# Three attention stages: projections into other PSUM banks, a minimum in place of score masks in level 0, and an order of its own for each level

## The reference

```python
# level 0: causal softmax attention        (level 2: the same without the mask, with its own layer norm)
q, k, v = (einsum('bsd,hdk->bhsk', x, W) + b for each of q, k, v)
scores = q @ k.T / sqrt(8)
scores = where(triu(ones, k=1), -1e9, scores)
out = (softmax(scores) @ v) @ Wo + bo
# level 3: rotated numerator, unrotated denominator, mask after the division
num = exp(rotate(q) @ rotate(k).T * scale)
den = sum(exp(q @ k.T * scale), axis=-1)        # over all keys
out = (where(tril, num / den, 0) @ v) @ Wout + bout
# around each:  x = x + attention(layernorm(x))
```

## Time and profile before

| | us |
|---|---|
| median of three runs | 5368.52 |
| the profiled execution | 5368.35 |
| its span | 5366.6 |
| level 0 attention, from first load to last addition | 274.2 to 502.9 |
| level 2 attention | 2768.7 to 3004.4 |
| level 3 attention | 4953.3 to 5176.4 |

### The profile page before, as it was taken

The page is one execution under the profiler, slowest core; times in us unless marked ns, Lnnn a source line. Parts: engine busy times, 40 slices in busy tenths (PEclk is TensorE's granted clock), DMA queues, the critical chain, the costliest instruction groups (busy, mean ns, idle before and its releaser), DMA issues. The chain is left out here.

```text
span 5366.6 us, 141783 instructions
## 1 busy us (share of the span) xinstructions
PE 4978.9 (93%) x49044; PEld 3454.0 (64%) x49044; DVE 3814.0 (71%) x7030; ACT 3438.1 (64%) x5879; POOL 2867.6 (53%) x3451
## 2 busy tenths in 40 slices
PE   8988977499999999999969699999999999989889
PEld 5655655267777777777745367777777777756556
DVE  2243236488888888888856488888888888845545
ACT  3333323278888888888845378888888888832642
POOL 0010005378788778778720288777787787700200
PEclk9989988599999999999979799999999999989899
DMA  1000000011111111112100111111111111110000
GB/s 44 1 5 34 1 1 9 29 45 55 51 50 51 55 51 49 51 51 55 43 15 1 40 39 55 51 51 49 55 51 55 46 55 51 39 34 7 1 25 9
DMA packets 110454, 195.51 MB, mean 36 GB/s; under 512 B 21409, under 2 KB 28849, under 8 KB 110257
## 3 DMA queue, kind: packets, MB, share of 16 engines
q1 hardware_dynamic: 110256, 192.82, 12.8%
HBM read 53.29 MB, written 1.05 MB: 10 GB/s over the span
## 5 line engine op out<-in xcount | busy, mean ns | idle before, releaser
L2674 POOL TENSOR_TENSOR stage_qk<-stage_halves 128x1024 f32<-128x1024 f32 x384 | 906.0, 2359 | 53.3 <-DVE stage_halves L2790 45.8
L2710 POOL TENSOR_TENSOR stage_qk<-stage_qk,stage_rnorm 128x1024 f32<-128x1024 f32 x384 | 730.9, 1903 | 30.5 <-issue 0.3
L2703 POOL TENSOR_TENSOR stage_probs<-stage_probs,stage_rsum 128x768 f32<-128x768 f32 x384 | 565.3, 1472 | 222.1 <-DVE stage_rsum L2819 209.6
L2787 DVE TENSOR_TENSOR stage_halves<-stage_wide,stage_tables 128x1024 f32<-128x1024 f32 x384 | 468.2, 1219 | 227.6 <-ACT stage_square L2493 187.4
L2493 ACT ACTIVATE stage_square<-stage_wide 128x1024 f32<-128x1024 f32 x384 | 394.0, 1026 | 191.9 <-PE stage_wide L2259 191.5
L2325 PE MATMUL stage_pv<-stage_probsT,stage_v_win 96*64 96x64 f32 x12288 | 488.1, 227 | 2.7 <-ACT stage_ctxT L2546 1.6
L2790 DVE TENSOR_TENSOR stage_halves<-stage_wide,stage_tables 128x512 f32<-128x512 f32 x768 | 490.5, 680 | 0.0
L2325 PEld LDWEIGHTS stage_pv<-stage_probsT,stage_v_win 96*64 96x64 f32 x12288 | 408.4, 137 | 122.7 <-issue 98.5
L2799 DVE TENSOR_REDUCE stage_norm<-stage_square 128x16 f32<-128x1024 f32 x384 | 464.7, 1210 | 30.8 <-issue 30.7
L2276 PE MATMUL stage_turn<-ident,stage_qk 128*128 128x128 f32 x3072 | 478.9, 279 | 4.9 <-ACT stage_qkT L2513 4.7
L2311 PEld LDWEIGHTS stage_flip<-ident,stage_probs 128*96 128x96 f32 x3072 | 355.6, 126 | 194.3 <-issue 130.0
(11 more groups left out here) (299 smaller groups left out, 9877.6 us busy)
## 6 DMA issues: line engine op xcount, KB each, us to landing
stage_v_win<-stage_v SPq DMA_DIRECT2D x384, 192.0 KB, 2.5
stage_v_win<-stage_v SPq DMA_DIRECT2D x384, 128.0 KB, 2.4
stage_v_win<-stage_v SPq DMA_DIRECT2D x192, 64.0 KB, 2.2
stage_wq<-in_T_wq SPq DMA_DIRECT2D x12, 512.0 KB, 4.1
stage_wk<-in_T_wk SPq DMA_DIRECT2D x12, 512.0 KB, 4.7
stage_wv<-in_T_wv SPq DMA_DIRECT2D x12, 512.0 KB, 3.5
stage_wo<-in_T_wo SPq DMA_DIRECT2D x12, 512.0 KB, 3.5
stage_w_up<-in_L_w_up SPq DMA_DIRECT2D x8, 512.0 KB, 6.6
```

The lines of the kernel that those rows point to most:

```text
L2674: nc.gpsimd.tensor_tensor(qk[:, n, :], halves[:, n % 2, 0, :], halves[:, n % 2, 1, :], ALU.add)\
L2703: nc.gpsimd.tensor_tensor(probs[:, m % 2], probs[:, m % 2], rsum[:, m % 2].to_broadcast([P, 2, 2 * HALVES, REACH]), ALU.mult)\
L2710: nc.gpsimd.tensor_tensor(heads, heads, rnorm[:, n, :].rearrange("p (h o) -> p h o", o=1).to_broadcast([P, LH, LD]), ALU.mult).then_inc(at ...
L2787: nc.vector.tensor_tensor(out[:, 0], heads, cos.to_broadcast([P, LH, LD]), ALU.mult)
```

## The change

1. **Banks.** `project` writes q and k to `pvT`. In level 3 the two swapped projections become a piece of their own, `project_swapped`, that writes to `turn`. `duo` then holds scores only. Waits follow: `weigh(…, 0)` waits for the projection to be read, `project` for `copy_weighed(…, 1)`, and the users of `turn` for `rotate` in level 3.
2. **Level 0.** `score` has no mask matmuls. The exponential is taken of all scores, and a new DVE piece, `keep_past`, takes the minimum of the two diagonal 128x128 blocks of each head with a constant (0 above the diagonal, the largest float on it and below). `weigh` waits for that (`kept`) and not for `probs`. `first_score` in level 0 and `score` in level 3 still write their masks by matmul.
3. **Orders.** Each level has its own `body` on each engine.
4. In level 3 `divide` waits for the sums of its own half only, and `read_projection` no longer waits for the scores three steps back (`rotate` does).

```diff
+    if level == 0:
+        per.update(kept=PAIRS)
...
+    usable = "kept" if cut else "probs"
...
+        diagonals = probs[:, :, :].rearrange("p h (b s) -> p h b s", s=P)[:, :, 0:3:2, :]
...
-                for n, w in enumerate([wq, wk] if softmax else [wq, wk, tiles["wq_swap"], tiles["wk_swap"]]):
-                    ins = nc.tensor.matmul(duo[:, n // 2, (n % 2) * SEQ:(n % 2 + 1) * SEQ], w[:, :], xT[:, :], start=True, stop=True)
+                for n, w in enumerate((wq, wk)):
+                    ins = nc.tensor.matmul(pvT[:, n, :], w[:, :], xT[:, :], start=True, stop=True)
                 ins.then_inc(sig["proj"], 1)
+
+            def project_swapped(step):
+                pe.wait_ge(*sig("xT", step, 1))
+                for n, w in enumerate((tiles["wq_swap"], tiles["wk_swap"])):
+                    ins = nc.tensor.matmul(turn[:, n * SEQ:(n + 1) * SEQ], w[:, :], xT[:, :], start=True, stop=True)
+                ins.then_inc(sig["swapped"], 1)
...
-                if causal:
+                if causal and not cut:
                     for side in range(2):
                         nc.tensor.matmul(kinds2(duo[:, side, :])[:, :, 0:P], ident_bf[:, :],
...
-                pe.wait_ge(*sig("probs", step, 2 * g + 2))
+                pe.wait_ge(*sig(usable, step, 2 * g + 2))
...
+            def keep_past(step, n):
+
+                dve.wait_ge(*sig("probs", step, n + 1))
+                own = diagonals[:, 2 * n:2 * n + 2]
+                limits = tiles["limits"].rearrange("p (h t s) -> p h t s", h=1, t=1).to_broadcast([P, 2, T, P])
+                nc.vector.tensor_tensor(own, own, limits, ALU.min).then_inc(sig["kept"], 1)
...
-                    dve.wait_ge(*sig("den", step, GROUPS))
+                    dve.wait_ge(*sig("den", step, 2 * half + 2))
...
+    a["A0_limits"] = np.where(above.T < 0, 0.0, np.finfo(np.float32).max).astype(np.float32)
```

More of the change, by code:

```diff
@@ L791 @@
 _last = [("bo", D), ("wo", D)]
[L792 removed]
+ATTN_PARTS = {0: _every + _softmax + [("limits", P)] + _last, 2: [("gamma", 1), ("beta", 1)] + _every + _softmax + _last,
               3: _every + [("wq_swap", D), ("wk_swap", D), ("rope", 2 * SEQ)] + _last}
@@ L866, in _, with bank_free @@
         def _(pe):
[L867 to L874, removed]
+            def bank_free(*before):
                 for name, step, count in before:
@@ L958, in score @@
                         ins = nc.tensor.matmul(duo[:, side, t * SEQ:(t + 1) * SEQ - first], key[:, t * P:(t + 1) * P],
-                                               query[:, first:SEQ], start=not causal, stop=True, skip_group_check=True)
+                                               query[:, first:SEQ], start=not causal or cut, stop=True, skip_group_check=True)
                 ins.then_inc(sig["scores"], 1)
@@ L1069, in _ @@
+            for s in range(-3, B + 3):
                 body(s)
@@ L1078, in copy_xT @@
                 act.wait_ge(*sig("v_psum", step))
+                if not softmax:
+                    act.wait_ge(*sig("swapped", step))
                 if level == 2:
@@ L1089, in read_projection @@
                     act.wait_ge(*sig("first_scores", step - ROOM + 1))
-                    act.wait_ge(*sig("scores", step - ROOM + 1))
+                    if softmax:
+                        act.wait_ge(*sig("scores", step - ROOM + 1))
                 if softmax:
@@ L1093, in read_projection @@
                         for n, (to, bias) in enumerate(((q_heads, tiles["bq"]), (k_heads, tiles["bk"]))):
-                            ins = nc.scalar.activation(to[:, step % ROOM, g, :], duo[:, 0, n * SEQ:(n + 1) * SEQ], ACT.Identity,
+                            ins = nc.scalar.activation(to[:, step % ROOM, g, :], pvT[:, n, :], ACT.Identity,
                                                        bias=bias[:, g:g + 1], scale=heads_of[:, g:g + 1])
@@ L1097, in read_projection @@
                 else:
-                    nc.scalar.activation(flat[:, step % ROOM, 0:2, :], kinds2(duo[:, 0, :]), ACT.Copy).then_inc(sig["flat"], 1)
+                    nc.scalar.activation(flat[:, step % ROOM, 0:2, :], pvT[:, :, :], ACT.Copy).then_inc(sig["flat"], 1)
             def denominators(step, g):
@@ L1205, in _, with body @@
                 nc.gpsimd.memset(v[:, :, :, :, DK:DK + 1], 1.0).then_inc(once["set"], 1)
-            def body(s):
-                if not softmax and runs(s):
-                    only_heads(s, 0)
-                if runs(s + 3):
-                    deviation(s + 3)
-                if not softmax and runs(s):
-                    only_heads(s, 1)
-                if runs(s + 2):
-                    add_bias(s + 2)
-                if level == 2 and runs(s + 3):
-                    second_deviation(s + 3)
-            for s in range(-3, B):
+            if level == 0:
+                def body(s):
+                    if runs(s + 2):
+                        add_bias(s + 2)
+                    if runs(s + 3):
+                        deviation(s + 3)
+            elif level == 2:
+                def body(s):
+                    if runs(s - 2):
+                        add_bias(s - 2)
+                    if runs(s):
+                        deviation(s)
+                    if runs(s - 1):
+                        second_deviation(s - 1)
+            else:
+                def body(s):
+                    if runs(s - 3):
+                        add_bias(s - 3)
+                    if runs(s + 1):
+                        only_heads(s + 1, 0)
+                    if runs(s + 1):
+                        only_heads(s + 1, 1)
+                    if runs(s + 3):
+                        deviation(s + 3)
+            for s in range(-3, B + 3):
                 body(s)
```

535 lines of the change are left out of this document (396 added, 139 removed).

## The result

The kernel after takes 5289.57 us (median of four runs, 5286.48 to 5293.0), the kernel before 5371.74 in the same comparison: a ratio of 0.9855, 95% interval 0.9839 to 0.9871. The forecast was 5294 us. The profiled execution took 5288.43 us, 79.9 less than that of before.

The account below looks back on a forecast made before the run. PE led, with waits from an equally long chain through `duo`. Savings of 16 us in fills, 42.4 in even steps and 15.9 in drains, 74.3 in all, took 5368.35 to 5294 us, range 5280 to 5306.

Parts of the forecast that it names:

- Banks, with the order: Projection leaves `duo`, so PE's work bounds even steps: 19.5, 21.6, 21.7 us in levels 0, 2, 3, masks' removal included.
- tight fit at `weigh(., 0)`: Level 0: last head copy ends about 5.6 us after the projection, and PE reaches the weighing 5.6 us after it.
- Masks to minima: Level 0's even steps: 2.6 us of masks leave PE per step; DVE gets eight minima, 5.5 us.
- DVE's slack: Level 0's even steps: DVE comes to 17.0 us of work (16.3 to 19.0) in a step of 19.5 us.
- Fills, level 0: Start of level 0, until step 3's projection: masks go, one piece comes, 3 us saved (bounds -4 and 12).
- the rival that I gave 0.17: Full clock comes sooner in fills or level 2's drain, each saving 7.5 us: 5272 us; chance 0.17.
- Fill, level 3: Five of ten first scores move behind step 3's projection, about 1.1 us each at half clock: 11 us saved (0 to 18).
- Drains: From step 7's projection on: 12.5 us saved in level 0, 6 in level 2, 2.6 lost in level 3.
- the projection's hold goes as well: Drains: the projection no longer occupies `duo`, saving 5.0 us in level 0, 5.5 in level 2, 5.2 in level 3.
- DVE did not lead: First rival: DVE leads in level 0, a step takes about 21.5 us, half a us more elsewhere: 5316 us; chance 0.15.
- `pvT` was no chain: Rival: PE stands at `weigh(., 0)` for head copies each step, so only masks' 21 us are saved: 5350 us; chance 0.08.
- the clock rose to 1.00 instead of falling: Rival: level 0's clock falls once full mask matmuls leave, a step costing 18.9 us more: 5389 us; chance 0.05.

Follow-up runs that it names:

- banks_only: Kernel before with q and k projections of levels 0 and 2 sent to `pvT`, every engine's old order kept: 5403.9 us, 1.006 of before.
- duo_again: Kernel after with the projections of levels 0 and 2 back in `duo` under the new order: 5414.16 us, 1.0083 of before.
- masks_back: Kernel after with level 0's score masks written by matmul again and no minima: 5316.85 us, 0.9894 of before.
- min_twice: Kernel after with every minimum of level 0 done twice, first into a spare tile: 5307.23 us, 0.9905 of before.
- min_only: Kernel before with level 0's score masks replaced by minima on DVE, old banks and PE order: 5356.35 us, 0.9971 of before.
- ahead3: Kernel after with level 3's first scores, their exponentials and sums one step earlier: 5310.12 us, 0.9898 of before.
- warm_first: Kernel after without level 0's first-score masks, with unread matmuls in level 0's fill and drain and level 2's fill: 5268.5 us, 0.9816 of before.
- warm: Kernel after with unread matmuls where PE would stand in fills and drains of levels 0 and 2: 5295.79 us, 0.988 of before.

## Why the prediction was right, and where it was not

- **Banks, with the order**: right. Steps of 19.3, 21.57 and 21.58 us where 19.5, 21.6 and 21.7 stood. That the price of a bank depends on the order is shown by `banks_only` and `duo_again`: in level 2's four steps it is worth 0.3 us in the old order and 44 in the new, of which some 33 come by the clock (the estimate above). Of the tight fit at `weigh(., 0)`, PE waited 0.2 us once in four steps.
- **Masks to minima**: right for the even steps. `masks_back` gives 2.7 us a step for the 2.6 counted. DVE's slack, 2.5 us by the count, is some 3 in `min_twice`. PE is the bound of level 0, but DVE is near: with the first scores' masks gone too, a step is 17.9 us, not 17.1. That DVE's fixed order is the reason is not shown.
- **Fills, level 0**: the term was mis-sized, 3 for 12.6. Twelve mask groups, in a fill partly at half clock, are worth 6.5 to 6.7, as `masks_back` (62.8 against 56.2) and `min_only` (62.1 against 68.9) both show. The rest goes with the clock, the rival that I gave 0.17; it held in the fills of levels 0 and 3, but not in that of level 2, whose clock fell from 0.69 to 0.66.
- **Fill, level 3**: the count was right, the price was not: 11 for 24.6. Five of ten first scores moved. An f32 matmul leaves two records, so a first score of 8 matmuls is x16 in the trace, and the fill has 160 before and 80 after (so what `ahead3` was expected to undo was also five, not ten). I took 11 us for their work alone and put the waits that stand ahead of them at nothing. Their work fell by 8.6 us (16.8 to 8.2), and PE's 8.3 us of idle time ahead of first scores, 6.1 of it for exponentials, went too. The last 7.7 us are PE's work on the other pieces, of which one score is gone and the rest run faster: the clock rose from 0.75 to 0.88. `ahead3` puts four first scores back, and with them 5.1 us of these waits and the clock at 0.76: 13.8 us. The rows of one first score and of the two fills, before and after:

```profile
4965.03 1.73 PE L926 MATMUL stage_quad<-stage_k_heads,stage_flat 32*128 32x256 f32 x16 [2.21 <-POOL stage_k_heads L1198]
```

```profile
L926 PE MATMUL stage_quad<-stage_k_heads,stage_flat 32*128 32x256 f32 x160 | 16.8, 496 | 8.3 <-ACT stage_den_exp L1104 6.1 <-POOL stage_k_heads L1198 2.2
```

```profile
L929 PE MATMUL stage_quad<-stage_k_heads,stage_flat 32*128 32x256 f32 x80 | 8.2, 399 | 0.0
```

- **Drains**: the step "the projection's hold goes as well" failed. A drain was priced by the chain through `duo`, but PE was busy for 60.2 of 68.6 us of level 2's, and other pieces filled the hold: PE waited 10.2 us for exponentials there before and 10.4 after. In level 0 PE had less to do (518 matmul records for 572), and the clock took it back: 23 us at half clock, with PE mostly busy, are up to 11 us (an estimate). At clock 0.95 the same code took 53.6 us (`ahead3`), and `warm_first`, at full clock and with fewer masks, 51.6, where I had 47.7; so the forecast of 12.5 saved was too high even at full clock. In level 3 the 5.1 lost would be 2.2 at full clock (61.3 us in `masks_back` and `min_twice`), for 2.6 forecast. That the idle left by a shorter chain lowers the clock fits `ahead3` and `duo_again`; it is not separated from chance, since drains of unchanged code moved by 3 to 6.5 us with the clock.
- **Rivals**: DVE did not lead, `pvT` was no chain, and in the even steps the clock rose to 1.00 instead of falling. The Trainium skill (TensorE: Matmul & The Clock Gate, HAM oscillation) says that gaps of PE re-throttle it; the runs agree, from 1.00 in the new even steps to 0.75 in those of `duo_again`.
- **Two small slips of the count**: PE was busy 90 to 92% of the even steps, not 91 to 92, and the first rival prices 12 steps of levels 2 and 3, which have 16. Neither moves a conclusion.

What stays open is which of a fill's waits tips the clock: the same instructions of level 2's fill gave 68.4 to 68.6 us in six kernels and 79.9 in one. Open too is what the banks and the order give apart in level 3's even steps.

## What to carry to other kernels

A bank freed is worth what the order puts between the pieces that share it; count what stands behind the new wait, and test bank and order together. Price even steps by the work of the engine that leads, but fills and drains by their clock as well: what a change saves there can be given back. When pieces leave a fill, price the waits ahead of them with their work. Run a kernel more than once before a few us of a fill or drain are read as an effect, and try a few unread matmuls where the fill waits.

## What the runs showed of the hardware

Half clock persists under load: in `warm`, level 2's fill from 2768 to 2792 us, PE was busy for 22.9 of 24 us at clock 0.50; it rose only some 3 us later.

```profile
2768.00:2792.00 24.00, 22.88 (x134) 0.50 0.00 1
```

DVE's normalisation of 128x128, 341 ns in level 0, averages 1167 in level 3's even steps of the kernel after, and did 338 before. The new order puts it beside POOL's spreading of keys. Of each pair, as the one below, one instruction takes 0.34 us and the other 2.0, about as long as POOL's whole instruction (1.89 us):

```profile
4947.56 2.25 DVE L1459 TENSOR_SCALAR stage_xn<-x_all,stage_norm_moments,stage_norm_rstd 128x128 f32<-128x128 f32 x2
...
4947.83 1.89 POOL L1402 TENSOR_TENSOR stage_k_heads<-stage_flat,stage_pack 128x1024 f32<-128x1024 f32 x1 [11.74 <-ACT stage_flat L1243]
```

The Trainium skill (SBUF — State Buffer, SBUF: two separate sides) says that a DVE instruction in a 2-port mode takes turns with GpSimd for whole instructions. The trace agrees in the length of the wait; no run shows the mode. In these steps DVE is busy for 61.7 of 86.3 us and PE for 83.8, so the wait is off the path that leads; no run tests what it costs.
